# A mixture-of-experts and recurrence kernel: the recurrence's rotation moved from ScalarE and GpSimd to VectorE, y copied out of PSUM by ScalarE and added by GpSimd, the second routing in two halves

## The chip, the core and the metric

One core of a Trainium2 chip runs the whole program. The metric is the device time of one execution in microseconds (us), here the median of several runs. Engines are named as in the profile: PE (TensorE), PEld (its weight loads), DVE (VectorE), ACT (ScalarE), POOL (GpSimd), SP (SyncE, which only issues transfers here).

## The reference

The input x has 8 batches of 512 rows of 128 numbers. Three layers follow each other, each with a residual connection and each behind a layer norm:

```
x = x + 0.5 * ffn(layernorm(x), gate_w, w1, w2)
x = x + attn(layernorm(x), a_params, B_w, C_w, D)
x = x + 0.5 * ffn(layernorm(x), gate_w, w1, w2)

attn:  Bu = u @ B_w.T;  h_t = real(ifft(lambdas * fft(h_{t-1}))) + Bu_t;  y_t = h_t @ C_w.T + D * u_t
ffn:   logits = tokens @ gate_w;  probs = softmax(logits);  expert = argmax(probs)    # 8 experts
       place of a token = how many earlier tokens chose the same expert; places of 160 and more are dropped
       out = probs[expert] * (relu(token @ w1[expert]) @ w2[expert])
```

## The kernel before

**Frame.** The 4096 rows are 32 tiles of 128 rows, four tiles to a batch. The kernel is one block of hand-written programs, one for each engine, each strictly in its own order; only semaphores (`wait_ge`, `then_inc`) order the engines against each other. There is no scheduler. The program has five stages: the first routing (gate logits, one-hot tables, a matmul that turns them into a token list), the first expert stage `slots(0)` (gather ten tiles of 128 slots by indirect DMA, two products for each of 8 experts, scatter back into a scratch copy of x in DRAM), the recurrence over the 8 batches, the second routing, and `slots(1)`. The text calls the pass of the recurrence loops for batch i "turn i".

**The recurrence.** The transform diagonalises the recurrence, so that a state is a complex number for each frequency, its real parts on partitions 0 to 63 and its imaginary parts on 64 to 127. Four consecutive rows form a group, and a batch has 128 groups. For batch b: DVE takes the layer norm's statistics (`stats`, `shift`), ACT the standard deviation (`deviation`) and the normalised rows u (`normalise`, four instructions); PE transposes u (`turn_u`), ACT copies it to SBUF (`copy_uT`); PE forms the group sums v in `bank[5]` (`group_sums`). v is turned back by the angle of its group: va = v * cosine on DVE (`turn_back`), and vb = v with its halves exchanged * sine, for which ACT copies the two halves of v crosswise into `vq` (`turned_part`) and POOL multiplies. DVE runs a cumulative sum over va and vb into z (`carry`) and turns z forth again: zs on DVE, zc on POOL, and state = zc + zs on DVE (`turn_forth`). PE adds the contribution inside the groups (`within_pairs`, `within_rest`) and that of the carried state (`read_out`) in one pair of PSUM banks, `pair[b % 2]`. That PSUM tile holds y and, beside it, the terms of the gate logits of the second routing. DVE reads both from PSUM: `add_back` (x2 = y + x1, which SP then sends to the output) and `gate_back` (the logits).

**Second routing.** It works on pieces of batches, `PIECES[1]`, here 0 to 2, 3 to 5, and 6 and 7. For a piece DVE finds each token's expert and counts (`mark`), PE adds the counts over partitions and earlier pieces (`rank`), DVE makes one-hot tables (`make_hot`), and PE multiplies them into one small PSUM tile (`place`); DVE makes the token list of it (`index(1)`), and POOL gathers with it after all rows of x2 are in DRAM (`d_out`). `keep_warm` is n matmuls of 128x512 whose result nobody reads.

Two orders matter. ACT, in turn i: `turned_part(i)`, `copy_uT(i + 1)`, `deviation(i + 2)`, `normalise(i + 2)`. DVE, in turn i: `turn_back(i)`, `stats(i + 2)`, `carry(i)`, `turn_forth(i)`, `add_back(i - 1)`, `gate_back(i - 1)`, `shift(i + 2)`, and then a part of the routing.

## Time and profile before

| quantity | value |
|---|---|
| time, median of 3 runs | 175.39 us (174.82 to 181.41) |
| the profiled execution: its time | 176.61 us |
| its span (first to last instruction) | 174.7 us |
| busy share of the span | PE 80%, PEld 60%, DVE 51%, ACT 33%, POOL 30% |
| the chain that ended last, by engine | PE 41%, DVE 24%, issue 10%, ACT 8%, DMA 8%, POOL 5% |

The table's time is that of the whole program, and the span is measured inside it; 1.9 us of the profiled execution lie outside its span. A row of the time line gives the start in us from the span's start, the length in us, the engine, the line of the kernel, the operation with output and inputs, and in square brackets how long the engine had been idle and what released it. Names are cut at their first digit, so that x stands for x1 and x2, and pair for all of PSUM. "x4" at a row's end says that four instructions in a row are merged.

### The profile page before, as it was taken

Reading aid. Unit: us, or ns where it says so; the run is one execution under the profiler, and the core shown is the slowest. Engines: PE = TensorE matmul, PEld = TensorE weight load, DVE = VectorE, ACT = ScalarE, POOL = GpSimd, SP = SyncE. Lnnn points to the kernel's source line nnn. Section 1 sums busy time; section 2 is a strip of 40 time slices with the busy share of each in tenths; the row PEclk is TensorE's granted clock in tenths of the full one; section 3 lists DMA queues with packets and bytes.
Section 4 is the critical chain, followed back from the end, with each engine's and each line's share of the span. In section 5 each row is a group of like instructions: output and inputs, shape, how many; then the busy total and the mean of one; then the engine's idle time right before and its main releaser. Section 6 shows DMA issues by size and latency. Waiting matters only on the chain.

```text
span 174.7 us, 2535 instructions
## 1 busy us (share of the span) xinstructions
PE 140.6 (80%) x788; PEld 104.8 (60%) x791; DVE 89.7 (51%) x396; ACT 58.2 (33%) x144; POOL 52.9 (30%) x80
## 2 busy tenths in 40 slices
PE   6977899989999787499788888896439969999920
PEld 2137468389998432388566666675234448999810
DVE  1069762984474206065485597698464134434320
ACT  3421143634736000846525525510000013483200
POOL 3700001776047720022012012121000477305771
PEclk9998589999999999999999999999555987999995
DMA  4999990111001129300101100111010011100110
GB/s 133 314 364 362 372 560 19 45 45 51 9 19 58 51 51 323 141 2 0 60 25 39 60 38 23 62 60 64 0 60 0 13 47 45 45 4 31 46 45 30
DMA packets 11309, 16.21 MB, mean 93 GB/s; under 512 B 1665, under 2 KB 6273, under 8 KB 11265
## 3 DMA queue, kind: packets, MB, share of 16 engines
q1 hardware_dynamic: 9504, 13.11, 21.4%
q0 software_dynamic: 1280, 2.62, 5.0%
q10 hardware_dynamic: 512, 0.33, 0.7%
q8 instruction: 6, 0.10, 0.2%
q14 instruction: 7, 0.05, 0.1%
HBM read 12.65 MB, written 5.51 MB: 104 GB/s over the span
## 4 chain that ended last, share of the span: by engine, by line
PE 41%; DVE 24%; issue 10%; ACT 8%; DMA 8%; POOL 5%; SPq 1%; POOLq 1%; DVEq 0%; ACTq 0%
PE pair L910 11%; PE pair L921 9%; ACT u L440 5%; PE pair L852 5%; DVE sstat L701 4%; PE pair L879 4%; DMA xt<-x_turned 3%; PE pair L804 3%; DVE x L748 2%; PE pair L899 2%; POOL zc L344 2%; DVE smv L706 2%; DVE z L730 2%; DMA x<-x_scratch 2%; DMA xg<-out,tok 2%
## 5 line engine op out<-in xcount | busy, mean ns | idle before, releaser
L804 PE MATMUL pair<-warm_in,ones_bf 128*128 128x512 bf16 x77 | 21.7, 428 | 4.2 <-DVE warm_in L469 1.6
L910 PE MATMUL pair<-xcT,w1s 128*128 128x160 f32 x128 | 21.8, 316 | 0.0
L921 PE MATMUL pair<-hT,w2s 128*128 128x160 f32 x128 | 20.5, 303 | 0.8 <-ACT hT L394 0.8
L910 PEld LDWEIGHTS pair<-xcT,w1s 128*128 128x128 f32 x128 | 18.9, 199 | 0.8 <-ACT xcT L386 0.8
L394 ACT ACTIVATE hT<-pair 128x320 f32<-128x320 f32 x32 | 13.7, 436 | 16.4 <-PE pair L910 15.0
L921 PEld LDWEIGHTS pair<-hT,w2s 128*128 128x128 f32 x128 | 18.1, 192 | 1.5 <-ACT hT L394 0.8
L440 ACT ACTIVATE u<-x,snb,srs 128x128 f32<-128x128 f32 x32 | 13.2, 482 | 13.4 <-DVE snb L716 13.4
L317 POOL DMA_INDIRECT xg<-x,tok x10 | 10.2, 1024 | 23.7 <-DVE tok L638 20.9
L317 POOL DMA_INDIRECT xg<-out,tok x10 | 10.1, 1006 | 22.0 <-DVE tok L638 19.2
L804 PEld LDWEIGHTS pair<-warm_in,ones_bf 128*128 128x128 bf16 x80 | 8.3, 110 | 13.7 <-issue 3.3
L386 ACT COPY xcT<-pair 128x128 f32<-128x128 f32 x20 | 4.9, 266 | 31.3 <-PE pair L894 31.2
L339 POOL TENSOR_TENSOR vb<-vq,st 128x128 f32<-128x128 f32 x8 | 3.6, 455 | 37.3 <-ACT vq L420 37.3
L1020 PE MATMUL pair<-gt,state 128*128 128x272 f32 x32 | 10.4, 453 | 3.8 <-DVE state L743 3.8
L326 POOL DMA_INDIRECT out<-xnew,tok x10 | 9.9, 988 | 10.7 <-DVE xnew L682 8.9
L326 POOL DMA_INDIRECT x_scratch<-xnew,tok x10 | 9.9, 986 | 9.8 <-DVE xnew L682 7.9
L645 DVE BATCH_NORM_STATS2 gstat<-xg 128x6 f32<-128x128 f32 x20 | 5.7, 287 | 12.4 <-DMA xg<-out,tok 9.2
L879 PEld LDWEIGHTS pair<-hot_tok,hot_place 128*64 128x64 f16 x64 | 7.4, 202 | 7.8 <-DVE hot_place L623 6.1
L879 PE MATMUL pair<-hot_tok,hot_place 128*64 128x20 f16 x64 | 7.8, 265 | 5.3 <-DVE hot_place L623 5.3
L701 DVE BATCH_NORM_STATS2 sstat<-x 128x6 f32<-128x128 f32 x32 | 6.9, 278 | 6.9 <-DMA x<-x_scratch 6.9
L722 DVE TENSOR_TENSOR va<-pair,ct 128x128 f32<-128x128 f32 x8 | 2.3, 291 | 15.1 <-ACT vq L420 15.1
L672 DVE COPY eoT<-pair 128x160 f32<-128x160 f32 x16 | 5.1, 318 | 9.3 <-PE pair L921 9.3
L852 PE MATMUL pair<-w1s,center 128*128 128x512 f32 x16 | 9.6, 754 | 0.0
(170 smaller groups left out, 247.1 us busy)
## 6 DMA issues: line engine op xcount, KB each, us to landing
xt<-x_turned SPq DMA_DIRECT2D x8, 256.0 KB, 6.0
w1s<-w SPq DMA_DIRECT2D x2, 1024.0 KB, 7.5
w2s<-w SPq DMA_DIRECT2D x8, 256.0 KB, 6.7
x<-x_scratch SPq DMA_DIRECT2D x8, 256.0 KB, 4.5
out<-x SPq DMA_DIRECT2D x8, 256.0 KB, 2.0
ce<-const_early ACTq DMA_DIRECT2D x1, 318.0 KB, 4.4
cl<-const_late SPq DMA_DIRECT2D x1, 256.0 KB, 5.5
xg<-x,tok POOLq DMA_INDIRECT x10, 2.6
```

Source lines behind the costliest of these rows:

```text
L317: pool.indirect_dma_start(xg[:, j, :], None, (x_rows, out_rows)[n], bass.IndirectOffsetOnAxis(ap=tok[:, j:j + 1], axis=0), bounds_check=T ...
L326: pool.indirect_dma_start((x1_dram, out_rows)[n], bass.IndirectOffsetOnAxis(ap=tok[:, j:j + 1], axis=0), xnew[:, j, :], None, bounds_check ...
L394: nc.scalar.activation(hT[:, e % 2, half * HC:(half + 1) * HC, :], bank[4 + half][:, 0:HC * CAP] .rearrange("p (c s) -> p c s", c=HC), ACT ...
L440: ins = nc.scalar.activation(u[:, b % 2, c, :], x1[:, b * TB + c, :], ACT.Identity, bias=snb[:, b % 2, c:c + 1], scale=srs[:, b % 2, c:c + 1])
L645: link(V.bn_stats(gstat[:, j, :], xg[:, j, :]))
L701: ins = V.bn_stats(sstat[:, b % 2, c, :], x1[:, b * TB + c, :])
L804: M(bank[to][:, :], ones_bf[:, :], warm_in[:, :], start=True, stop=True)
L852: M(bank[e % 2][:, :], center[:, :], w1s[:, e, :], start=True, stop=True).then_inc(w1c_ps, 1)
L879: ins = M(bank[7][0:SW, 0:NSTRIP], hot_place[:, :, t], hot_tok[:, :, t], start=(t == 0), stop=(t == NT - 1))
L910: ins = M(bank[4 + half][:, c * CAP:(c + 1) * CAP], w1s[:, i, ch * P:(ch + 1) * P], xcT[:, i * CAP:(i + 1) * CAP], start=True, stop=True)
L921: ins = M(bank[6 + i % 2][:, 0:CAP], w2s[:, i, c, :], hT[:, i % 2, c, :], start=(c == 0), stop=(c == FC - 1))
L1020: ins = M(y[:, h, E:E + 2 * PITCH], state[:, b % 2, :], gt[:, 2 * h:2 * h + 2, :].rearrange("p r c -> p (r c)"), start=False, stop=True, s ...
```

## The change

In the recurrence, DVE computes vb itself: two instructions of 64 partitions each read v in PSUM and write the other half. ACT's two crosswise copies and POOL's product go; the cumulative sum subtracts vb. ACT gets a new step, `copy_y`, that copies y and the logit terms of a batch (128x576) from PSUM to SBUF (`yb`). `add_back` moves from DVE to POOL and `gate_back` stays on DVE, both now reading `yb`. On ACT `deviation` stands ahead of `copy_uT` instead of behind it. The second routing works on two pieces of four batches. The logits of the last batch no longer come out of its y: PE forms them by their own products (`gates_within`, `gates_carried`) from tables `tg` that POOL makes between its first gathers and first scatters (`first_tables`), and DVE reads them in `gate_first`. `keep_warm` ahead of `slots(1)` is one call of 14, in place of calls of 8 and 16 around the last `place`.

```diff
-    PIECES = [[(0, NB)], [(0, 3), (3, 6), (6, NB)]]
+    PIECES = [[(0, NB)], [(0, NB // 2), (NB // 2, NB)]]
+    LAST = NB - 1
+    YW = 2 * E + 2 * PITCH
...
-            return [(t0, (t0 + t1) // 2), ((t0 + t1) // 2, t1)] if n == 0 else [(t0, t1)]
+            return [(t0, (t0 + t1) // 2), ((t0 + t1) // 2, t1)]
...
-            for b in range(NB):
-                pool.wait_ge(vq_sb, b + 1)
-                if b >= 1:
-                    pool.wait_ge(z_r, b)
-                nc.gpsimd.tensor_tensor(vb[:, :], vq[:, :], st[:, 0:NG], ALU.mult).then_inc(vb_r, 1)
+            def first_tables():
+                pool.wait_ge(out_table, 1)
+                link(nc.gpsimd.memset(tg[:, :, :, :], 0.0))
+                for k in range(TB):
+                    nc.gpsimd.tensor_copy(tg[:, k, 0, k * E:].rearrange("p (j e) -> p j e", e=E),
+                                          tab[:, E:E + PITCH * (TB - k)].rearrange("p (j c) -> p j c", c=PITCH)
+                                          [:, :, D:PITCH])
+                    ins = nc.gpsimd.tensor_copy(tg[:, k, 1, k * E:(k + 1) * E], gate_c[:, 0:E])
+                ins.then_inc(first_table, 1)
...
+            def add_back(b):
+                pool.wait_ge(y_sb, b + 1)
+                nc.gpsimd.tensor_tensor(x2[:, b * TB:(b + 1) * TB, :].rearrange("p (h r) d -> p h r d", h=2),
+                                        y_copy(b)[:, :, :, 0:D],
+                                        x1[:, b * TB:(b + 1) * TB, :].rearrange("p (h r) d -> p h r d", h=2),
+                                        ALU.add).then_inc(x2_r, 1)
+            gather(0)
+            first_tables()
+            scatter(0)
+            pool.wait_ge(turns, 1)
+            for i in range(NB):
+                turn_cosine(i)
+                if i >= 1:
+                    add_back(i - 1)
+            add_back(LAST)
...
-            def turned_part(b):
-                act.wait_ge(v_ps, b + 1)
-                if b >= 1:
-                    act.wait_ge(vb_r, b)
-                v = bank[5][:, 0:NG]
-                nc.scalar.copy(vq[0:P // 2, :], v[P // 2:P, :])
-                nc.scalar.copy(vq[P // 2:P, :], v[0:P // 2, :]).then_inc(vq_sb, 1)
+            def copy_y(b):
+                act.wait_ge(y_ps, b + 1)
+                if b >= 2:
+                    act.wait_ge(x2_r, b - 1)
+                    act.wait_ge(y_read, b - 1)
+                nc.scalar.copy(yb[:, b % 2, :, :], y_pair(b)[:, :, 0:YW]).then_inc(y_sb, 1)
...
             for i in range(NB):
-                turned_part(i)
+                if i >= 1:
+                    copy_y(i - 1)
+                if i + 2 < NB:
+                    deviation(i + 2)
                 if i + 1 < NB:
                     copy_uT(i + 1)
                 if i + 2 < NB:
-                    deviation(i + 2)
                     normalise(i + 2)
+            copy_y(LAST)
...
             def turn_back(b):
-                dve.wait_ge(vq_sb, b + 1)
-                V.tensor_tensor(va[:, :], bank[5][:, 0:NG], ct[:, 0:NG], ALU.mult).then_inc(va_r, 1)
+                dve.wait_ge(v_ps, b + 1)
+                V.tensor_tensor(va[:, :], bank[5][:, 0:NG], ct[:, 0:NG], ALU.mult)
+                for src, dst in halves:
+                    ins = V.tensor_tensor(vb[dst, :], bank[5][src, 0:NG], st[src, 0:NG], ALU.mult)
+                ins.then_inc(va_r, 1)
...
+            def gate_first():
+                dve.wait_ge(first_ps, 1)
+                dve.wait_ge(y_read, LAST)
+                link(V.tensor_tensor(lgu[:, :, :], first[:, 1, :, :],
+                                     ssd[:, LAST % 4, :].unsqueeze(2).broadcast_to([P, TB, E]), ALU.mult))
+                V.tensor_tensor(lgs[:, LAST * TB:NT, :], first[:, 0, :, :], lgu[:, :, :], ALU.add).then_inc(y_read, 1)
...
-                if i == ROUTE_FROM:
+                if i == NB // 2:
                     mark(1, 0, (True, False))
-                if i == ROUTE_FROM + 1:
+                if i == NB // 2 + 1:
                     mark(1, 0, (False, True))
-                if i == ROUTE_FROM + 2:
-                    make_hot(1, 0, (True, False))
-                if i == ROUTE_FROM + 3:
-                    make_hot(1, 0, (False, True))
+                if i == NB // 2 + 2:
+                    make_hot(1, 0)
+            gate_first()
             mark(1, 1)
-            gate_back(NB - 1)
-            mark(1, 2)
-            add_back(NB - 1)
             make_hot(1, 1)
-            make_hot(1, 2)
             index(1)
...
+            def gates_within(b):
+                pe.wait_ge(first_table, 1)
+                pe.wait_ge(va_r, b + 1)
+                for k in range(TB):
+                    M(bank[5][:, 256:256 + 2 * TB * E], uT[:, b % 2, k * P:(k + 1) * P],
+                      tg[:, k, :, :].rearrange("p k c -> p (k c)"), start=(k == 0), stop=False, skip_group_check=True)
+            def gates_carried(b):
+                pe.wait_ge(state_r, b + 1)
+                M(first[:, 0, :, :], state[:, b % 2, :], gt[:, :, D:PITCH], start=False, stop=True,
+                  skip_group_check=True).then_inc(first_ps, 1)
...
+            group_sums(LAST)
+            read_out(LAST - 1)
+            gates_within(LAST)
+            gates_carried(LAST)
+            within_pairs(LAST)
+            within_rest(LAST)
             rank(1, 1)
-            read_out(NB - 1)
+            read_out(LAST)
+            place(1, 0)
             place(1, 1)
-            rank(1, 2)
-            keep_warm(8, 0)
-            place(1, 2)
-            keep_warm(16, 0)
+            keep_warm(14, 0)
             slots(1)
```

The order of ACT's instructions in turn 3, first before and then after. vq is the crosswise copy of v, yb the copy of y, ssd the deviation, uT the transposed u, u the normalised rows of the batch two turns ahead.

```order
L419 COPY vq<-pair 64x128 [waits vb_r,v_ps]
L420 COPY vq<-pair 64x128
L427 COPY uT<-pair 128x512 [waits lag_ps,uT_ps]
L433 ACTIVATE ssd<-smv,eps 128x4 [waits y_read,svar]
L440 ACTIVATE u<-x,snb,srs 128x128 [waits uT_ps,snb_r]
L440 ACTIVATE u<-x,snb,srs 128x128 x3
```

```order
L444 COPY yb<-pair 128x576 [waits y_read,x2_r,y_ps]
L457 ACTIVATE ssd<-smv,eps 128x4 [waits y_read,svar]
L451 COPY uT<-pair 128x512 [waits lag_ps,uT_ps]
L464 ACTIVATE u<-x,snb,srs 128x128 [waits uT_ps,snb_r]
L464 ACTIVATE u<-x,snb,srs 128x128 x3
```

The two copies that stood behind the preceding turn's u are gone, and no instruction of ACT stands between v and DVE any more.

DVE in turn 3, before and then after, from the first product on v to the first instruction of `gate_back`.

```order
L722 TENSOR_TENSOR va<-pair,ct 128x128 [waits vq_sb]
L701 BN_STATS sstat<-x 128x6 [waits d_x1_5]
...
L743 TENSOR_TENSOR state<-zc,zs 128x128 [waits y_ps,zc_r,zs_r]
L748 TENSOR_TENSOR x<-pair,x 128x512 [waits y_ps]
L758 TENSOR_TENSOR lgu<-pair,ssd 128x2x8 [waits y_ps]
```

```order
L751 TENSOR_TENSOR va<-pair,ct 128x128 [waits v_ps]
L753 TENSOR_TENSOR vb<-pair,st 64x128 x2
L728 BN_STATS sstat<-x 128x6 [waits d_x1_5]
...
L773 TENSOR_TENSOR state<-zc,zs 128x128 [waits y_ps,zc_r,zs_r]
L781 TENSOR_TENSOR lgu<-yb,ssd 128x2x8 [waits y_sb]
```

The first product waits for PE's sums instead of ACT's copy, two products of 64 partitions are new, and the 128x512 addition is gone.

PE from the group sums of the last batch to the first product of the last piece's one-hot tables, before and then after. counted belongs to `rank`, hot_tok and hot_place to `place`, tg to `gates_within`.

```order
L1020 MATMUL pair<-gt,state 128x272 [waits state_r]
...
L1012 MATMUL pair<-tab,uT 128x144
L879 MATMUL pair<-hot_tok,hot_place 64x20 [waits hot]
L879 MATMUL pair<-hot_tok,hot_place 64x20 x11
L864 MATMUL pair<-counted_0,ones_bf 128x96 [waits rank_read,marked]
...
L1020 MATMUL pair<-gt,state 128x272 [waits state_r]
L1020 MATMUL pair<-gt,state 128x272
L879 MATMUL pair<-hot_tok,hot_place 64x20 [waits hot]
L879 MATMUL pair<-hot_tok,hot_place 64x20 x11
L864 MATMUL pair<-counted_0,ones_bf 128x64 [waits rank_read,marked]
```

```order
L1054 MATMUL pair<-tg,uT 128x64 [waits va_r,first_table]
L1054 MATMUL pair<-tg,uT 128x64 x3
L1060 MATMUL pair<-gt,state 128x32 [waits state_r]
L1021 MATMUL pair<-tab,uT 128x280 [waits y_sb]
...
L1036 MATMUL pair<-tab,uT 128x144
L889 MATMUL pair<-counted_0,ones_bf 128x128 [waits rank_read,marked]
...
L1044 MATMUL pair<-gt,state 128x272 [waits state_r]
L1044 MATMUL pair<-gt,state 128x272
L904 MATMUL pair<-hot_tok,hot_place 64x20 [waits hot]
L904 MATMUL pair<-hot_tok,hot_place 64x20 x7
```

The small gate products now stand ahead of the last batch's other products and wait for its state, the last `rank` stands ahead of the last `read_out`, and every `place` of the second routing stands behind it.

## Rows read from the trace of the kernel before

**Rows 1.** Time line of DVE, va of turn 3, then turn 4.
```profile
93.52 0.29 DVE L722 TENSOR_TENSOR va<-pair,ct 128x128 f32<-128x128 f32 x1 [2.27 <-ACT vq L420]
...
100.05 0.29 DVE L722 TENSOR_TENSOR va<-pair,ct 128x128 f32<-128x128 f32 x1 [1.89 <-ACT vq L420]
100.26 0.86 DVE L701 BATCH_NORM_STATS2 sstat<-x 128x6 f32<-128x128 f32 x4
...
101.45 0.39 DVE L730 TENSOR_TENSOR_SCAN z<-va,vb 128x128 f32<-128x128 f32 x1
101.87 0.75 DVE L734 TENSOR_TENSOR zs<-z,st 64x128 f32<-64x128 f32 x2
102.66 0.29 DVE L743 TENSOR_TENSOR state<-zc,zs 128x128 f32<-128x128 f32 x1
102.86 0.68 DVE L748 TENSOR_TENSOR x<-pair,x 128x512 f32<-128x512 f32 x1
103.46 0.25 DVE L758 TENSOR_TENSOR lgu<-pair,ssd 128x16 f32<-128x16 f32 x2
...
104.06 0.16 DVE L716 SCALAR_TENSOR_TENSOR snb<-smv,srs 128x4 f32<-128x4 f32 x1
```

**Rows 2.** Time line of ACT, end of turn 3 and turn 4.
```profile
97.74 1.65 ACT L440 ACTIVATE u<-x,snb,srs 128x128 f32<-128x128 f32 x4 [2.40 <-DVE snb L716]
99.41 0.26 ACT L419 COPY vq<-pair 64x128 f32<-64x128 f32 x1
...
100.13 0.59 ACT L427 COPY uT<-pair 128x512 f32<-128x512 f32 x1 [0.19 <-PE pair L977]
101.56 0.30 ACT L433 ACTIVATE ssd<-smv,eps 128x4 f32<-128x4 f32 x1 [0.84 <-DVE smv L706]
```

**Rows 3.** Time line of PE, group sums of turns 1 and 2, and the read out between.
```profile
76.86 1.05 PE L986 MATMUL pair<-uT,vt 128*128 128x128 f32 x8
78.11 1.18 PE L1020 MATMUL pair<-gt,state 128*128 128x272 f32 x4 [0.20 <-DVE state L743]
...
81.92 1.05 PE L986 MATMUL pair<-uT,vt 128*128 128x128 f32 x8
```

**Rows 4.** Time line of DVE behind the last turn.
```profile
118.64 0.29 DVE L743 TENSOR_TENSOR state<-zc,zs 128x128 f32<-128x128 f32 x1
...
124.37 0.26 DVE L758 TENSOR_TENSOR lgu<-pair,ssd 128x16 f32<-128x16 f32 x2 [2.47 <-PE pair L1020]
...
131.55 0.23 DVE L604 TENSOR_TENSOR own_count<-pair,chosen 128x64 f32<-128x64 f32 x1 [1.95 <-PE pair L871]
...
135.95 0.17 DVE L631 TENSOR_SCALAR unfilled<-pair 64x20 f32<-64x20 f32 x1 [2.25 <-PE pair L879]
```

**Rows 5.** Time line of PE behind the last turn.
```profile
122.19 2.15 PE L1020 MATMUL pair<-gt,state 128*128 128x272 f32 x4
...
131.73 3.19 PE L804 MATMUL pair<-warm_in,ones_bf 128*128 128x512 bf16 x7 [0.22 <-issue]
```

**Rows 6.** Busy time by stretch: PE, PEld, DVE, ACT, POOL, granted clock, DMA, GB/s.
```profile
122.00:123.00 1.00, 1.00 (x6) 0.88 (x7) 0.00 (x0) 0.00 (x0) 0.00 (x0) 0.53 0.00 0
```

**Rows 7.** Groups by form on POOL: busy us, mean ns, idle before.
```profile
L344 POOL TENSOR_TENSOR zc<-z,ct 128x128 f32<-128x128 f32 x8 | 4.5, 559 | 10.5 <-DVE z L730 10.5
L339 POOL TENSOR_TENSOR vb<-vq,st 128x128 f32<-128x128 f32 x8 | 3.6, 455 | 37.3 <-ACT vq L420 37.3
```

**Rows 8.** Groups by form on DVE, columns as in rows 7.
```profile
L551 DVE TENSOR_TENSOR chosen<-key,top_key 128x128 bf16<-128x128 bf16 x2 | 1.4, 716 | 0.1
L623 DVE TENSOR_TENSOR hot_place<-split_i,place_no 128x512 f16<-128x512 int16 x1 | 0.4, 416 | 0.0
```

**Rows 9.** The chain that ended last, first routing: start, us, what.
```profile
24.37 3.63 PE pair L879 x32
```

**Rows 10.** Time line of POOL, the first scatter.
```profile
49.94 1.01 POOL L326 DMA_INDIRECT x_scratch<-xnew,tok  x1 [7.04 <-DVE xnew L682]
```

**Rows 11.** The page's list of DMA issues: count, KB each, us to landing.
```profile
out<-x SPq DMA_DIRECT2D x8, 256.0 KB, 2.0
```

50 lines of the change are left out of this document (19 added, 31 removed).

## The prediction

> **What bounds the kernel now.** I read the chain of waits first. Outside the two expert stages, which the diff leaves alone, it runs through the recurrence and the second routing; so I read the time lines of the engines there.
>
> *A turn of the recurrence* takes 6.53 us, from the va of turn 3 at 93.52 to that of turn 4 at 100.05, and DVE stood idle for 1.89 us before the latter, released by ACT's vq copy [rows 1]. ACT was late because vq stands behind the four u instructions of batch 5 (97.74, 1.65 us), and these had waited 2.40 us for DVE's snb [rows 2]. The snb of a turn comes last on DVE, 104.06 + 0.16 = 4.17 us behind its va [rows 1]. So the turn is one ring: va, statistics, z, zs, state, x2, logits, snb on DVE (4.2 us), then u and vq on ACT (2.3 us). The reader is to see that v itself has long been ready; the ring closes only because ACT is strictly in order.
>
> *PE's own work* in a turn is shorter. From the group sums of turn 1 (76.86) to those of turn 2 (81.92) are 5.06 us with 0.20 us of waiting for the state [rows 3]: 4.9 us of work. A turn therefore wastes some 1.6 us.
>
> *Behind the last turn* the state is ready at 118.64 + 0.29 = 118.93, and the token list starts at 135.95 [rows 4]: 17.0 us. DVE waits three times there for PE: 2.47 us for the last read_out, 1.95 us for the last rank, 2.25 us for the last place [rows 4]. The read_out took 2.15 us at a granted clock of 0.50 to 0.53, PE's lower level of 1.2 GHz, against 1.18 us at 2.4 GHz [rows 3, 5, 6], and eight keep_warm products (3.19 us for seven recorded) still ran when the last one-hot table was done [rows 5].
>
> **The change part by part.**
>
> *Out of the ring.* va now waits for PE's sums alone. Then what comes last in a turn? DVE's turn from the row starts [rows 1]: va 0.21, statistics to z 1.19, z 0.42, zs 0.79, state 0.20, then (x2's 0.60 is gone) logits and shift 0.60 to the start of snb and some 0.08 until the next instruction starts: 3.5 us. New is vb, two products of 64 partitions out of PSUM. The trace has no such pair; the nearest are the two zs, 64 partitions crosswise, 0.75 us [rows 1], and va, 0.29 us for 128 partitions out of PSUM, started 0.21 us apart. So 0.42 to 0.85 us; I take 0.70, nearer to zs, as that is the same crosswise form. DVE: 4.2 us. ACT: y copy of 576 columns at the uT copy's rate, 0.59 x 576 / 512 = 0.66, deviation 0.30, uT 0.59, u 1.65 [rows 2]: 3.2 us. POOL: zc 0.56 and x2, four times the columns of a product that takes 0.455 alone and 0.559 beside DVE's zs [rows 7]: 1.2 (part of the 0.455 is start-up) to 2.24 us, so 1.8 to 2.8 us. PE's 4.9 us is the largest, and **PE bounds the turn**.
>
> Do the orders allow it? Counted from the group sums of turn i: sums done 1.05, va to svar until 3.1, snb until 5.2, u of batch i + 2 until 6.9. PE wants that u for its transposes 3.4 us into the next turn, at 8.3: 1.4 us to spare. The state is ready at 4.5 or so and wanted at 1.05 of the next turn, 5.95. The read_out of the turn before ends at 2.25, the y copy at 2.95, deviation (behind svar) at 3.4, the transposes of u at 4.0, the uT copy at 4.65, wanted at 4.9. That last one has the least to spare, 0.25 us. What is queued behind the y copy on ACT is deviation, uT and u; behind deviation's wait stands uT. Only in turn 0 does this show: deviation there comes later than uT's wait and pushes it by some 0.25 us. POOL's x2 starts at 4.1 and ends at 6.3 at the latest, before the next z at 8.4.
>
> So group sums of turn 1 at 77.1, of turn 5 at 77.1 + 4 x 4.9 = 96.7.
>
> *Routing inside the loop.* The first piece now has 16 tiles instead of 12. Turn 4 gets two small instructions (0.6 us), which DVE's spare 0.7 us takes. Turn 5 gets the choice: 0.72 for `chosen` [rows 8], its neighbours some 0.25, 0.3 and 0.4, 1.7 us in all, and from there DVE is last. Its va of turn 5 is at 96.7 + 1.1 = 97.8; with 4.2 and 1.7 turn 6 starts at 103.7. Turn 6 has no statistics: 2.8 us, then the whole make_hot. Two hot_place at 0.42 [rows 8] and nine small ones of 0.1 to 0.4 make 2.85. Turn 7 starts at 109.35; va and vb 1.0 with their wait, z 0.46, zs 0.79 and state 0.29 [rows 1] make the state of batch 7 ready at **111.9**, where it was 118.9: 7.0 us gained.
>
> *Behind the state.* gates_carried on PE 0.35 (read_out's four large products take 1.18 [rows 3], so this one small one at most a third), gate_first 0.45 (two instructions like lgu's, each waited for [rows 1]), mark on 16 tiles 2.4 (the 0.6 and 1.7 from above with their waits), all in a row: 115.1. PE does the products inside the groups meanwhile (2.4 us) and is free at about 114.7. rank, four small products and no row of that size here: between 0.3 and half of read_out, taken as 0.5: 115.6. Now two branches. DVE: make_hot, 2.85, done at 118.45. PE: read_out 1.1 to 116.7, then place of all 32 tiles, 3.63 in the first routing [rows 9], to **120.35**. PE is last. Before, 17.0 us lay between the state and the list; now 8.45.
>
> *Other work that is moved.* first_tables stands on POOL ahead of the first scatter, where POOL idled for 7.04 us [rows 10]. It is nine instructions of 8 to 256 columns, under 0.3 us each: at most 2.7 us, hidden; its cover is the wait for the first expert's rows. The x2 of batch 7 now goes y copy on ACT (0.66), POOL (1.2 to 2.24), then the transfer that lands after 2.0 us [rows 11]: 116.7 + 0.05 + 0.66 + 1.7 + 2.07 = 121.2. The gathers also need the list itself, 0.9 us behind 120.35, at 121.25. So it is hidden by nothing to spare; at POOL's upper bound it costs 0.5 us. Before, that transfer was long done.
>
> *POOL beside DVE.* zc takes 0.559 beside DVE's zs, vb 0.455 without [rows 7], and the two zs together take 0.75 where two starts 0.29 apart would give 0.6 [rows 1]. x2 on POOL now lies beside state, logits and snb in each turn and beside turn 7's. In the turns DVE has room; in the chain from turn 5 on I add 0.4 us. The Trainium skill (GPSIMD Engine Reference, Specifications) says that POOL's SBUF interface is shared with VectorE and that they contend when the VectorE instruction has two SBUF inputs; its section on engine selection advises against elementwise work with two inputs on GpSimd. The rows fit with that: both sides are longer where they overlap. By that rule the 0.4 us stays; were the overlap free, the sum would be 0.4 us lower.
>
> **Sum.** 135.95 - 120.35 = 15.6 gained, less 0.4: 15.2 us. Everything behind the list is unchanged in the diff but for fewer warming products. The profiled execution of 176.61 us would take 161.4. It was 1.2 us above the median of the runs, 175.39, so for a median I forecast **160.4 us**.
>
> **Rivals.**
>
> *A, the clock.* PE's clock was at its lower level from 122 on [rows 6], behind two microseconds in which PE had nearly no work. In the changed kernel PE works without a gap until about 109, then waits for DVE's turn 7, does 0.5 us of gate products and waits again until 112.2. If the level falls there, the products inside the groups take 4.8 instead of 2.4 us and end at 117.1 instead of 114.7; rank then is 1.5 us later, read_out takes 1.0 us more [rows 3, 5], and the sum loses some 2.5, perhaps 4 with what the warming takes: 163.5. For it: nearly 2.5 us of idling in a stretch of 3. Against it: in the turns before, PE idled 1.3 us of each 6.5 and kept its clock.
>
> *B, a longer turn.* Another wait takes the ring's place: ACT's uT copy, which has 0.25 us to spare, or DVE slowed by POOL. A turn of 5.6 instead of 4.9 costs 0.7 x 5 = 3.5 us: 164. For it: 0.25 us is little, and waits between engines cost some 0.05 each. Against it: no single row contradicts the times.
>
> *C, faster still.* vb at its lower bound and the overlap free give 0.3 x 3 + 0.4 = 1.3 us; and the warming products end nearer to the first gathered tile, so that the expert stage may start at the full clock: 1 us or so. 158.5.
>
> *D, slower than before.* POOL becomes the bound: x2 is a product of 512 columns, and if DVE keeps POOL from SBUF much more than zc shows, a turn is zc plus x2. It breaks even when seven turns give back 15.2 us, that is a turn of 4.9 + 2.2 = 7.1 us and an x2 of 6.5 us, three times its upper bound of 2.24 [rows 7]. At 8 us for x2 the time would be about 186. Only a contention of which no row shows a sign would do it.
>
> *E, the gate products bring nothing.* The last mark would wait as before for the last y: 2.4 + 1.1 us behind the state instead of 0.35, less what rank no longer has to wait: about 2.5 us, 163. The order shows that they stand ahead, so only their table or the bank they share could delay them.
>
> **How the numbers follow.** The forecast as worked out has 0.55, A 0.17, B 0.14, C 0.09, E 0.03, D 0.02. The likeliest is the forecast: 160.4. For the range, C's end and the bounds of vb and x2 below (158.3), and A and B above, with one and a half us for both at once: 165.5. Two per cent, about what a measurement of this kernel can tell from no change, is 3.5 us; every case but D is faster by far more. Faster 0.96, same 0.02, slower 0.02.
>
> **What would show it.** Right: va released by PE's sums, not by ACT; group sums some 4.9 us apart with PE idle under 0.3 us a turn; DVE last from turn 5; list at about 120 to 121; place right behind read_out with no keep_warm between; x2 on POOL 1.2 to 2.2 us. Wrong: a turn over 5.4 us (B), granted clock 0.5 between 111 and 118 (A), gathers that start later than 0.9 us behind the list because the last output is still on its way.

## The result, and the profile after

The changed kernel took 168.26 us (median of four runs, 166.73 to 169.68) against 176.44 us for the kernel before beside it: a ratio of 0.9528, 95% interval [0.9456, 0.9601]. Four more executions of it on another occasion gave 168.04 us and 0.9464 [0.9355, 0.9574]. It is faster by 5%, where 8.5% were forecast; 168.26 lies above the range. The profiled execution took 166.96 us with a span of 165.1, so it is compared with the forecast of 161.4: 5.6 us are missing.

The time line of DVE in turns 2 and 3 of the changed kernel (columns as in [rows 1], which these answer):

```profile
77.10 0.29 DVE L773 TENSOR_TENSOR state<-zc,zs 128x128 f32<-128x128 f32 x1
...
83.96 0.28 DVE L751 TENSOR_TENSOR va<-pair,ct 128x128 f32<-128x128 f32 x1
84.26 0.59 DVE L753 TENSOR_TENSOR vb<-pair,st 64x128 f32<-64x128 f32 x2
...
86.51 0.76 DVE L764 TENSOR_TENSOR zs<-z,st 64x128 f32<-64x128 f32 x2
87.30 1.25 DVE L773 TENSOR_TENSOR state<-zc,zs 128x128 f32<-128x128 f32 x1
...
89.15 0.28 DVE L751 TENSOR_TENSOR va<-pair,ct 128x128 f32<-128x128 f32 x1
```

and that of POOL beside it:

```profile
86.55 0.56 POOL L351 TENSOR_TENSOR zc<-z,ct 128x128 f32<-128x128 f32 x1 [3.34 <-DVE z L761]
87.08 1.32 POOL L356 TENSOR_TENSOR x<-yb,x 128x512 f32<-128x512 f32 x1
...
123.60 1.29 POOL L356 TENSOR_TENSOR x<-yb,x 128x512 f32<-128x512 f32 x1 [6.72 <-ACT yb L444]
```

The ring is gone: va follows at once, where it had waited for vq [rows 1]. But the turn is 5.19 us (83.96 to 89.15), and DVE has no idle time in it: DVE bounds it, not PE. One row grew. The addition that makes `state` takes 1.25 us in every turn with an x2 beside it, and 0.29 us in turn 0 (77.10), the only one without. It ends at 88.55, 0.15 us behind the end of POOL's x2 at 88.40. (The profile calls its times on POOL rough; experiments 2 to 5 show whether this distance holds for other instructions.)

PE of the changed kernel, group sums of turns 1, 2 and 7, the read_out behind the first of them and products behind the last; then its clock by stretch (columns as in [rows 6]):

```profile
77.68 1.05 PE L1011 MATMUL pair<-uT,vt 128*128 128x128 f32 x8
78.57 1.08 PE L1044 MATMUL pair<-gt,state 128*128 128x272 f32 x4
...
82.28 1.05 PE L1011 MATMUL pair<-uT,vt 128*128 128x128 f32 x8
...
109.20 1.05 PE L1011 MATMUL pair<-uT,vt 128*128 128x128 f32 x8
...
114.66 1.94 PE L1054 MATMUL pair<-tg,uT 128*128 128x64 f32 x8 [2.88 <-DVE vb L753]
...
117.53 1.28 PE L1021 MATMUL pair<-tab,uT 128*128 128x280 f32 x2
...
121.50 0.22 PE L889 MATMUL pair<-counted,ones_bf 128*128 128x128 bf16 x1
```
```profile
74.00:78.00 4.00, 4.00 (x19) 3.46 (x18) 3.47 (x17) 1.17 (x3) 0.49 (x1) 0.71 0.01 2
...
114.00:117.00 3.00, 1.94 (x8) 1.78 (x8) 2.87 (x7) 0.00 (x0) 1.83 (x2) 0.50 0.00 0
120.00:122.00 2.00, 2.00 (x13) 1.69 (x13) 0.66 (x3) 0.00 (x0) 0.00 (x0) 0.84 0.03 8
```

Unhindered, PE's turn is 4.60 us (77.68 to 82.28). In turn 7 PE had waited 2.88 us for DVE, and its clock stood at the lower level, 1.2 GHz, so that its products inside the groups ended only near 121.5. In 74 to 78 the clock had also been low for a part.

DVE behind the last turn of the changed kernel, answering to [rows 4]:

```profile
115.79 1.24 DVE L773 TENSOR_TENSOR state<-zc,zs 128x128 f32<-128x128 f32 x1
...
121.91 0.29 DVE L631 TENSOR_TENSOR own_count<-pair,chosen 128x128 f32<-128x128 f32 x1 [1.31 <-PE pair L896]
...
123.42 0.33 DVE L645 TENSOR_TENSOR hot_strip<-split_i,strip_no 128x320 f16<-128x320 int16 x1
123.78 1.29 DVE L647 TENSOR_TENSOR hot_tok<-hot_strip,token_half 128x320 f16<-128x320 f16 x1
...
127.43 0.17 DVE L658 TENSOR_SCALAR unfilled<-pair 64x20 f32<-64x20 f32 x1 [1.70 <-PE pair L904]
```

`hot_tok`, of the size of `hot_strip` (0.33 us), takes 1.29 us, because x2 of the last batch lies beside it (123.60 to 124.89). The list starts at 127.43. The first gather starts 1.76 us behind it (129.19), where it was 1.75 before; so the last output doesn't hold the gathers up, and the 0.9 us that the prediction took for this step were too few in both kernels.

Traces differ by a microsecond or three in when the recurrence begins, for reasons upstream of the diff. So from here on the yardstick is the **stage**: from the start of the recurrence's first statistics on DVE to the start of the list (`unfilled`). Before it was 135.95 - 66.53 = 69.42 us; changed, 127.43 - 65.68 = 61.75; forecast, 120.75 - 66.53 = 54.2. That is a gain of 7.7 where 15.2 were forecast; 0.85 and 1.1 us came from upstream and from behind the list.

| profiled execution | stage | to the last state | state to list | turn | state | group sums 0 to 1 |
|---|---|---|---|---|---|---|
| before | 69.42 | 52.11 | 17.31 | 6.45 | 0.29 | 3.78 |
| forecast | 54.2 | 45.1 | 9.1 | 4.9 | | |
| changed | 61.75 | 50.11 | 11.64 | 5.19 | 1.25 | 5.46 |
| changed, again (12) | 61.78 | 49.05 | 12.73 | 5.18 | 1.24 | 4.27 |
| changed, warmed ahead of the tail (8) | 63.00 | 51.41 | 11.59 | 5.18 | 1.25 | 6.43 |
| changed, first turn warmed (11) | 61.79 | 49.06 | 12.73 | 5.19 | 1.25 | 4.26 |
| x2 on DVE (1) | 58.87 | 49.14 | 9.73 | 4.84 | 0.29 | 6.61 |
| the same without own gate products (7) | 60.24 | 49.12 | 11.12 | 4.84 | 0.29 | 6.48 |
| x2 later on POOL (2) | 57.47 | 46.92 | 10.55 | 4.60 | 0.29 | 4.26 |
| x2 in four on POOL (3) | 58.20 | 47.98 | 10.22 | 4.87 | 0.43 | 5.47 |
| x2 and tables later (9) | 57.94 | 47.00 | 10.94 | 4.60 | 0.29 | 6.50 |
| the same, first turn warmed (10) | 54.35 | 44.66 | 9.69 | 4.60 | 0.29 | 4.26 |
| rotation alone (6) | 63.21 | 47.14 | 16.07 | 4.83 | 0.29 | 5.46 |
| before, dose on POOL (4) | 73.85 | 57.05 | 16.80 | 7.17 | 1.01 | 5.47 |
| before, copy on POOL (5) | 70.44 | 54.03 | 16.41 | 6.74 | 0.58 | 3.78 |

"To the last state" and "state to list" split the stage at the start of the last `state`; the turn is turn 2, from va to va; the numbers in brackets are those of the experiments. The last column tells TensorE's clock in the first turn. At 3.78 (kernel before) and 4.3 us it was full. At 5.5 us it was at the lower level for some 3 us, and at 6.4 to 6.6 us for some 6. Rows with a like last column can be compared. Some executions of every kernel run at a lower granted clock and take longer: the medians below count them, the ratios leave them out, and the profiled executions of experiments 1, 7 and 9 are such (167.28, 169.09 and 167.59 us), which shows ahead of the first statistics and in the first turn.

### The profile page after: what moved, and what is told of

Same layout as the page of the kernel before. It is cut to its first block, busy times and chain, and to the rows that moved or that the text cites. A ratio compares the mean times of both kernels' runs of the same rounds, so it can differ in the third digit from the quotient of the medians.

```text
span 165.1 us, 2502 instructions
## 1 busy us (share of the span) xinstructions
PE 140.3 (85%) x783; PEld 107.7 (65%) x786; DVE 95.4 (58%) x389; ACT 58.3 (35%) x136; POOL 60.7 (37%) x87
## 4 chain that ended last, share of the span: by engine, by line
PE 40%; DVE 28%; issue 9%; POOL 9%; DMA 8%; ACT 2%; POOLq 1%; SPq 0%; DVEq 0%
PE pair L935 8%; PE pair L946 8%; PE pair L877 5%; DVE state L773 5%; DVE sstat L728 4%; POOL xg L321 4%; PE pair L904 3%; DMA xt<-x_turned 3%; POOL zc L351 2%; DVE vb L753 2%; PE pair L924 2%; DMA x<-x_scratch 2%; PE pair L849 2%; DMA xg<-out,tok 2%; DVE z L761 2%
## 5 line engine op out<-in xcount | busy, mean ns | idle before, releaser
L829 PE MATMUL pair<-warm_in,ones_bf 128*128 128x512 bf16 x67 | 19.0, 431 | 4.3 <-DMA x<-x_scratch 1.6
L935 PE MATMUL pair<-xcT,w1s 128*128 128x160 f32 x128 | 20.7, 305 | 0.0
L351 POOL TENSOR_TENSOR zc<-z,ct 128x128 f32<-128x128 f32 x8 | 4.4, 551 | 41.9 <-DVE z L761 41.9
L935 PEld LDWEIGHTS pair<-xcT,w1s 128*128 128x128 f32 x128 | 18.0, 190 | 0.8 <-ACT xcT L411 0.8
L829 PEld LDWEIGHTS pair<-warm_in,ones_bf 128*128 128x128 bf16 x70 | 7.4, 111 | 13.3 <-issue 4.0
L356 POOL TENSOR_TENSOR x<-yb,x 128x512 f32<-128x512 f32 x8 | 10.5, 1309 | 6.7 <-ACT yb L444 6.7
L1044 PE MATMUL pair<-gt,state 128*128 128x272 f32 x32 | 9.3, 414 | 1.1 <-DVE state L773 0.8
L444 ACT COPY yb<-pair 128x576 f32<-128x576 f32 x8 | 5.0, 624 | 14.0 <-PE pair L1044 14.0
L1011 PE MATMUL pair<-uT,vt 128*128 128x128 f32 x64 | 9.0, 285 | 0.7 <-ACT uT L451 0.7
L709 DVE SCALAR_TENSOR_TENSOR xnew<-pair,gscale,xg 128x128 f32<-128x128 f32 x20 | 6.4, 346 | 5.3 <-PE pair L955 5.2
```

The lines of the kernel that those rows point to most:

```text
L356: nc.gpsimd.tensor_tensor(x2[:, b * TB:(b + 1) * TB, :].rearrange("p (h r) d -> p h r d", h=2), y_copy(b)[:, :, :, 0:D], x1[:, b * TB:(b + ...
L829: M(bank[to][:, :], ones_bf[:, :], warm_in[:, :], start=True, stop=True)
L935: ins = M(bank[4 + half][:, c * CAP:(c + 1) * CAP], w1s[:, i, ch * P:(ch + 1) * P], xcT[:, i * CAP:(i + 1) * CAP], start=True, stop=True)
L1011: ins = M(bank[5][:, 0:NG], vt[:, TB - 1 - c, :], uT[:, b % 2, c * P:(c + 1) * P], start=(c == 0), stop=(c == TB - 1))
L1044: ins = M(y[:, h, E:E + 2 * PITCH], state[:, b % 2, :], gt[:, 2 * h:2 * h + 2, :].rearrange("p r c -> p (r c)"), start=False, stop=True, s ...
```

## The experiments

Each median stands beside runs of the kernel before on the same chip. Diffs are cut to the lines that matter, with `...` for what is left out inside a line or between lines.

**1. x2 on DVE.**

```diff
             def add_back(b):          # moved from POOL's program to DVE's
-                pool.wait_ge(y_sb, b + 1)
-                nc.gpsimd.tensor_tensor(x2[...], y_copy(b)[...], x1[...], ALU.add).then_inc(x2_r, 1)
+                dve.wait_ge(y_sb, b + 1)
+                V.tensor_tensor(x2[...], y_copy(b)[...], x1[...], ALU.add).then_inc(x2_r, 1)
...
             make_hot(1, 1)
+            add_back(LAST)
```

> x2 of every batch back on DVE (reading the copy yb), the rest of the change kept; the last x2 stands behind the last make_hot. Theory H (hold): a DVE instruction with two inputs in SBUF that is issued while POOL runs its 128x512 addition ends only when that addition has ended; in the changed kernel this made state 1.25 us long instead of 0.29 and hot_tok 1.29 instead of 0.32. H expects state at 0.29 us and hot_tok at 0.32 in this run; DVE loses 0.95 and regains 0.60 per turn, so the turn falls from 5.19 to about 4.85 us, turns 5 to 7 give 0.35 each, the last table 0.7: time 2 to 3 us below the changed kernel's 166.9, about 164.5. Rival R (the length of state has another cause, such as its inputs or the semaphores it waits for): state stays at 1.25 us and the turn grows by 0.60, time about 171. Rival S (shared rate: DVE and POOL each run slower while both read SBUF): state 0.29 as well, but see the run with four small additions.

Measured: 163.69 us, ratio 0.9283 [0.9179, 0.9387]. DVE's time line of this kernel:

```profile
91.35 0.29 DVE L763 TENSOR_TENSOR state<-zc,zs 128x128 f32<-128x128 f32 x1
91.56 0.69 DVE L768 TENSOR_TENSOR x<-yb,x 128x512 f32<-128x512 f32 x1
...
97.69 0.28 DVE L741 TENSOR_TENSOR va<-pair,ct 128x128 f32<-128x128 f32 x1
```

`state` is back at 0.29 us and the last `hot_tok` at 0.33, and the turn is 4.84 (the va before stands at 92.85) although DVE does one more instruction of 0.69: moving x2 to POOL cost DVE more (0.95) than the 0.60 us that it saved. The stage is 2.9 us shorter than in the changed kernel's first trace, although the first turn's clock was worse. Against experiment 8, the changed kernel with a like first turn, it is 4.1 us shorter.

**2. x2 on POOL, but later**: behind snb of its turn, so that it runs beside the next va, vb and statistics; the last one on DVE.

```diff
                 turn_cosine(i)
+                if 1 <= i and i + 2 < NB:
+                    pool.wait_ge(snb_r, i + 3)
+                if i + 2 == NB:
+                    pool.wait_ge(rank_read, piece(1, 0) + 1)
+                if i + 1 == NB:
+                    pool.wait_ge(y_read, LAST)
                 if i >= 1:
                     add_back(i - 1)
-            add_back(LAST)
...
             make_hot(1, 1)
+            add_last(LAST)     # DVE: the x2 of the last batch
```

> x2 stays on POOL but starts later: in turns 1 to 5 behind DVE's snb, so that it lies beside va, vb and the statistics, which read at most one input from SBUF; in turn 6 behind own_count, in turn 7 behind gate_back; the last x2 is on DVE behind the last make_hot. H expects state at 0.29 us in every turn, none of va, vb or the statistics longer than before, DVE's turn 4.2 us and PE the bound at 4.7 to 4.9 us a turn; 0.3 to 0.5 us for each of turns 2 to 5, 0.95 for each of turns 5 to 7, 0.7 behind the last rank: time 4 to 5 us below the changed kernel, about 162.5. S expects that the time which state loses comes back on va, vb and the statistics, so a turn of 5.1 us and a time within 1 us of the changed kernel. R expects no change of state and no gain.

Measured: 164.0 us, ratio 0.93 [0.9156, 0.9444]. POOL and DVE of this kernel, turns 3 and 4, then three rows of the routing:

```profile
92.87 1.27 POOL L356 TENSOR_TENSOR x<-yb,x 128x512 f32<-128x512 f32 x1 [1.24 <-DVE snb L748]
...
97.47 1.27 POOL L356 TENSOR_TENSOR x<-yb,x 128x512 f32<-128x512 f32 x1 [1.24 <-DVE snb L748]
```
```profile
91.81 0.29 DVE L778 TENSOR_TENSOR state<-zc,zs 128x128 f32<-128x128 f32 x1
...
93.06 0.29 DVE L756 TENSOR_TENSOR va<-pair,ct 128x128 f32<-128x128 f32 x1 [0.27 <-PE pair L1025]
93.37 0.59 DVE L758 TENSOR_TENSOR vb<-pair,st 64x128 f32<-64x128 f32 x2
93.99 0.87 DVE L733 BATCH_NORM_STATS2 sstat<-x 128x6 f32<-128x128 f32 x4
...
97.62 1.27 DVE L573 TENSOR_TENSOR is_top<-lgs,top 128x128 bf16<-128x128 f32 x1
...
103.92 1.43 DVE L583 TENSOR_TENSOR chosen<-key,top_key 128x128 bf16<-128x128 bf16 x1
...
109.21 0.93 DVE L640 TENSOR_SCALAR over<-count 128x16 f32<-128x16 f32 x1
```

Now va has to wait 0.27 us for PE, and a turn is 4.60 us: PE bounds it, as forecast, and faster than forecast. Beside va and vb (one input in PSUM) and the statistics (one input; all of them lie beside x2 in turn 5 of experiment 10), POOL's x2 lengthens nothing: 0.29, 0.59 and 0.87 us as without. Where it meets `is_top`, with two inputs in SBUF, that takes 1.27 instead of 0.29, and again ends just behind it (98.89, and 98.74). `chosen` (1.43 for 0.70) and `over` (0.93 for 0.17, one input in SBUF) are held too, so part of the gain is lost in the routing. They don't end 0.15 us behind POOL (104.77 and 110.11) but 0.58 and 0.03. What is common to all of them is the difference: each ends its own unhindered time, less 0.12 to 0.14 us, behind the end of POOL's instruction. A held instruction thus does nearly all of its work afterwards. The stage is 4.3 us shorter than that of experiment 12, the changed kernel with the same full clock in the first turn.

**3. x2 on POOL as four additions of 128x128** in the place of one.

```diff
-                nc.gpsimd.tensor_tensor(x2[...], y_copy(b)[:, :, :, 0:D], x1[...], ALU.add).then_inc(x2_r, 1)
+                for h in range(2):
+                    for r in range(2):
+                        ins = nc.gpsimd.tensor_tensor(x2[:, b * TB + 2 * h + r, :], y_copy(b)[:, h, r, 0:D],
+                                                      x1[:, b * TB + 2 * h + r, :], ALU.add)
+                ins.then_inc(x2_r, 1)
```

> x2 on POOL at its place in the changed kernel, but as four additions of 128x128 instead of one of 128x512. H, if the hold lasts for one POOL instruction: state gets in between two of them and takes 0.3 to 0.8 us instead of 1.25; the turn falls by 0.3 us or more to PE's bound, time 1.5 to 3.5 us below the changed kernel, 163.5 to 165.5. S expects state unchanged at 1.1 to 1.3 us, since the same number of elements is read, and the time unchanged or up to 1 us longer for the added starts.

Measured: 166.86 us, ratio 0.9482 [0.9159, 0.9805]; the interval is wide, the trace is clear. POOL, then DVE:

```profile
87.41 1.81 POOL L358 TENSOR_TENSOR x<-yb,x 128x128 f32<-128x128 f32 x4
```
```profile
87.63 0.43 DVE L774 TENSOR_TENSOR state<-zc,zs 128x128 f32<-128x128 f32 x1
87.98 0.51 DVE L782 TENSOR_TENSOR lgu<-yb,ssd 128x16 f32<-128x16 f32 x2
```

POOL reads the same data for longer, 1.81 us, yet DVE loses less: `state` 0.43, lgu 0.51 for 0.25. So DVE isn't slowed in proportion to POOL's traffic; it is kept out until the instruction in hand ends, and gets in between two. The stage is 3.6 us shorter than in the changed kernel's first trace, whose first turn was alike.

**4. The dose on the kernel before**: a POOL addition of 128x512 behind each zc, whose result nobody reads.

```diff
                 nc.gpsimd.tensor_tensor(zc[:, :], z[:, 0:NG], ct[:, 0:NG], ALU.mult).then_inc(zc_r, 1)
+                nc.gpsimd.tensor_tensor(spare[:, :, :], x1[:, b * TB:(b + 1) * TB, :], x1[:, b * TB:(b + 1) * TB, :],
+                                        ALU.add)
```

> The kernel before, with one more instruction on POOL in each turn: a 128x512 addition of two SBUF operands into a tile that nobody reads, right behind zc, so that it lies beside DVE's state. Theory H (a VectorE instruction with two SBUF inputs issued beside it ends only when it has ended): state goes from 0.29 to about 1.25 us in all 8 turns though nothing waits for POOL's result; the ring grows by 0.95 and the time by 0.95 x 8 = 7.6 us, 6.5 to 8. Rival S (shared rate): state 0.4 to 0.6 and the time 1 to 3 us longer. Rival R (state is long in the changed kernel for a reason of its own): no change of state and of the time.

Measured: 181.78 us (179.53 to 186.51) beside 177.95 for the kernel before (175.81 to 179.59), less than expected; stage 139.84 - 65.99 = 73.85. DVE and POOL:

```profile
90.58 1.01 DVE L746 TENSOR_TENSOR state<-zc,zs 128x128 f32<-128x128 f32 x1
```
```profile
90.36 1.08 POOL L346 TENSOR_TENSOR spare<-x 128x512 f32<-128x512 f32 x1
```

One instruction without a reader makes `state` 1.01 us and the turn 7.17 (va at 87.97 and 95.14) instead of 6.45: both are 0.72 us longer. Up to the last `state` there are seven such turns, 5.0 us, and the trace is 4.9 us longer there. The expected 7.6 us took the dose for as long as x2; it is 0.2 us shorter, and the part behind the last `state` is 0.5 us shorter than before, since the clock fell later there (DVE waits 1.60 us for the last read_out instead of 2.47). The hold needs nothing else of the change.

**5. A copy in place of that addition**, one input instead of two.

```diff
-                nc.gpsimd.tensor_tensor(spare[:, :, :], x1[:, b * TB:(b + 1) * TB, :], x1[:, b * TB:(b + 1) * TB, :],
-                                        ALU.add)
+                nc.gpsimd.tensor_copy(spare[:, :, :], x1[:, b * TB:(b + 1) * TB, :])
```

> The kernel before, with one more POOL instruction behind each zc: a copy of 128 x 512 values of x1 into a spare tile, that is, one input where the addition of the earlier dose had two. Its result is used by nobody. Theory H (any POOL instruction on this much data keeps DVE out while it runs): state takes 0.29 us plus what is left of the copy, near 1 us, as beside the addition (1.01 us). Theory T (POOL has to read two inputs for it): state stays at 0.29 us, and the turns at 6.5 us, as in the kernel before.

Measured, one execution: 177.72 us beside 176.67.

```profile
96.75 0.67 POOL L346 COPY spare<-x 128x512 f32<-128x512 f32 x1
```
```profile
96.98 0.58 DVE L745 TENSOR_TENSOR state<-zc,zs 128x128 f32<-128x128 f32 x1
```

The copy is shorter than I had allowed for, and `state` again ends 0.14 us behind it (97.56, and 97.42). It is 0.29 us longer than alone; seven times that is 2.0 us, and up to the last `state` the trace is 1.9 us longer. Theory H holds as against T: a copy with one input holds `state` as an addition does, for as long as it runs.

**6. The rotation alone**: the kernel before with vb on DVE, without ACT's copies and POOL's product, and without the rest of the change.

```diff
-                turned_part(i)
...
-                dve.wait_ge(vq_sb, b + 1)
-                V.tensor_tensor(va[:, :], bank[5][:, 0:NG], ct[:, 0:NG], ALU.mult).then_inc(va_r, 1)
+                dve.wait_ge(v_ps, b + 1)
+                V.tensor_tensor(va[:, :], bank[5][:, 0:NG], ct[:, 0:NG], ALU.mult)
+                for h in range(2):
+                    src, dst = slice((1 - h) * P // 2, (2 - h) * P // 2), slice(h * P // 2, (h + 1) * P // 2)
+                    ins = V.tensor_tensor(vb[dst, :], bank[5][src, 0:NG], st[src, 0:NG], ALU.mult)
+                ins.then_inc(va_r, 1)
```

> The kernel before with one part of the change: DVE computes vb out of PSUM in two instructions, ACT's crosswise copies and POOL's product are gone; x2 stays on DVE out of PSUM, the routing stays in three pieces. Theory P (the ring over ACT was the bound): the turn falls from 6.5 to 4.7 to 4.9 us, DVE's work of 4.8 us beside PE's of 4.6 to 4.9, and since no POOL addition lies beside state this one part alone gains 8 to 10 us, as much as the whole change does: 166 to 168. Rival: freeing DVE of x2 was the needed part, and DVE with vb and x2 has turns of 5.3 us or more, a gain under 6 us.

Measured: 169.57 us, ratio 0.9532 [0.9424, 0.964]; stage 128.93 - 65.72 = 63.21. This part alone gives what the whole change gives, within the intervals. Up to the last `state` it is 3.0 us quicker than the changed kernel, at the same low clock in the first turn; behind it 4.4 us slower. So what the change does for the second routing gains behind the turns. Of the 3.0 us that it loses in them, the holds account for 2.1 to 2.3 (experiments 1 and 2 up to the last `state`, against 8 and 12); the rest isn't assigned by any run. Turn 2 falls from 6.45 to 4.83 us, and DVE has no idle time in it: with x2 still on DVE, DVE bounds the turn and not PE.

**7. The last batch's logits out of its y again**, on the kernel with x2 on DVE.

```diff
-            gate_first()
+            dve.wait_ge(y_read, LAST)
+            gate_back(LAST)
...
-            gates_within(LAST)
-            gates_carried(LAST)
...
-            rank(1, 1)
             read_out(LAST)
+            rank(1, 1)
```

> The kernel with x2 on DVE, but the last batch's logits come out of its y again: gates_within and gates_carried go, read_out of the last batch stands ahead of the last rank, and gate_back(LAST) takes the place of gate_first. Theory P (the own gate products bring what they were forecast to, since the last mark no longer waits for y): own_count of the last half comes some 2.5 to 3 us later behind the last state than in the run with x2 on DVE (there 5.12 us behind the start of state), the list as well, and the median goes from 163.7 to about 166.3. Theory E (they bring nothing, PE's products inside the groups decide anyway): own_count and the median stay within 0.5 us.

Measured: 165.23 us, ratio 0.9322 [0.9238, 0.9406], against 0.9283 with the products: 1.5 us in the medians, inside both intervals. Its trace has own_count 6.51 us behind the last `state`:

```profile
118.37 0.29 DVE L763 TENSOR_TENSOR state<-zc,zs 128x128 f32<-128x128 f32 x1
...
121.30 0.26 DVE L779 TENSOR_TENSOR lgu<-yb,ssd 128x16 f32<-128x16 f32 x2 [1.64 <-ACT yb L434]
...
124.88 0.29 DVE L621 TENSOR_TENSOR own_count<-pair,chosen 128x128 f32<-128x128 f32 x1 [0.68 <-PE pair L897]
```

With the products it was 123.08 - 117.96 = 5.12. So they bring some 1.4 us, neither 2.5 to 3 nor nothing. Without them DVE waits for y only 1.64 us, because PE has done the products inside the groups before the state comes (the last ends at 116.44). Both tails had the lower clock for a part, this one longer (its read_out took 1.81 us, 1.08 at full clock), so at one clock it would be less.

**8. Twelve warming products behind the last but one read_out**, in the changed kernel, for PE's waiting ahead of its gate products.

```diff
             read_out(LAST - 1)
+            keep_warm(12, 4)
             gates_within(LAST)
```

> The changed kernel with keep_warm(12) on PE between read_out of batch 6 and gates_within, where PE idled for 2.88 us and its granted clock then was 0.50 until 121. Theory C (the lower clock cost time in the tail): the clock stays at 1.0 until the last rank, gates_within takes 0.9 instead of 1.94 us, the products inside the groups 2.6 instead of 4.0, the last rank no longer waits for them (DVE idles 0.5 instead of 1.31 us before own_count): the time falls by 0.8 to 1.5 us. Rival: the tail is set by DVE alone, and the time does not change by more than 0.3 us; or the warming products run into the gate products and cost up to 0.5 us.

Measured: 172.25 us, ratio 0.9747 [0.9563, 0.9931]. PE and its clock (of PE alone: length, busy time, granted clock, DMA share, GB/s):

```profile
120.44 1.08 PE L1054 MATMUL pair<-tg,uT 128*128 128x64 f32 x8 [0.30 <-DVE vb L753]
122.86 0.41 PE L1060 MATMUL pair<-gt,state 128*128 128x32 f32 x2 [1.35 <-DVE state L773]
...
123.90 1.11 PE L1023 MATMUL pair<-tab,uT 128*128 128x272 f32 x2
```
```profile
120.00:123.00 3.00, 1.35 (x11) 1.00 0.00 0
123.00:126.00 3.00, 3.00 (x10) 0.57 0.25 93
```

The gate products now run at full clock (1.08 for 1.94 us), but they did so without the warming as well, in experiments 11 and 12. But PE waits 1.35 us more for the `state` that POOL holds up, and then the clock falls for the products inside the groups. own_count comes 6.07 us behind the start of `state`, 6.12 without the warming: nothing gained there. The stage was 63.0, with the first turn at half clock, and the first statistics were 4.5 us later (70.16) than in the changed kernel, upstream of the edit. This is time lost ahead of the edit, so the slower median can't be put down to the warming; why all four executions (171.08 to 176.15) are slower than seven of the changed kernel's eight (166.73 to 169.68, the eighth 171.60), one trace can't say. Theory C fell: filling that one gap doesn't keep the clock.

**9. x2 later, and the second half of the first piece's tables behind the last mark.** On the kernel of experiment 2, with x2 of batch 3 waiting for the next va instead of snb:

```diff
-                    make_hot(1, 0)
+                    make_hot(1, 0, (True, False))
...
             mark(1, 1)
+            make_hot(1, 0, (False, True))
             make_hot(1, 1)
```

> The changed kernel with x2 moved as in the earlier run, the one of turn 4 now beside the statistics of turn 5, and with the first piece's make_hot cut in two: own_count to split_i in turn 6, the tables themselves behind the last mark, where DVE idled 1.3 to 1.9 us for the last rank. Theory: the state of batch 7 is ready 1.5 us earlier, PE idles 1.5 us less before its gate products, the wait for the last rank is filled; 1.5 to 2.5 us faster than the run with x2 moved alone, about 161.5 to 162.5. Rival: PE's lower clock in the tail returns the gain, since the last rank waits for PE's products: less than 0.5 us.

Measured: 165.5 us, ratio 0.9236 [0.9099, 0.9373]. The stage was 57.94, against 57.47 in experiment 2, but here the first turn ran at the lower clock and there at the full one. Experiment 10 gives the fair comparison: the same schedule with a full first turn reaches the last `state` in 44.66 us, experiment 2 in 46.92. Of these 2.3 us, 1.0 come from the x2 of batch 3, which no longer holds `is_top` (from the state of turn 4 to that of turn 5 are 4.89 us for 5.86), and 1.3 from the later tables (5.03 us for 6.31 from turn 6 to 7). The expectation was 1.5.

**10. The same kernel with 22 instead of 14 warming products ahead of the first turn.**

```diff
             pe.wait_ge(d_x1[0], 16)
-            keep_warm(14, 6)
+            keep_warm(22, 6)
             turn_u(0)
```

> The kernel with x2 later on POOL and its tables behind the last mark (median 165.5 in its run), with 22 instead of 14 warming products ahead of the first turn, so that PE works until the first u is ready instead of idling some 2 us. Theory W (the idling of those 2 us is what lets the granted clock fall in the first turn): the first group sums take 1.16 us or less in place of 2.08, group sums 1 start 4.3 us behind group sums 0 instead of 6.5 (4.26 and 6.50 are the two that earlier runs showed), and the median falls to about 163. Theory U (the clock falls by what happened earlier, whatever PE does in those 2 us): the first turn shows 0.50 to 0.6 again in this run where it did in the others, and the median stays at 164 to 165.5.

Measured: **160.88 us**, ratio 0.9101 [0.903, 0.9173], the fastest of all; its six runs span 160.41 to 163.49. PE, DVE and the clock:

```profile
67.03 4.92 PE L846 MATMUL pair<-warm_in,ones_bf 128*128 128x512 bf16 x22 [1.55 <-DMA x<-x_scratch]
...
73.56 1.16 PE L1028 MATMUL pair<-uT,vt 128*128 128x128 f32 x8 [0.68 <-ACT uT L458]
```
```profile
111.67 0.29 DVE L780 TENSOR_TENSOR state<-zc,zs 128x128 f32<-128x128 f32 x1
...
116.79 0.28 DVE L638 TENSOR_TENSOR own_count<-pair,chosen 128x128 f32<-128x128 f32 x1
...
121.36 0.17 DVE L665 TENSOR_SCALAR unfilled<-pair 64x20 f32<-64x20 f32 x1 [1.09 <-PE pair L921]
```
```profile
114.00:117.00 3.00, 2.17 (x14) 1.44 (x12) 2.86 (x9) 0.00 (x0) 0.00 (x0) 1.00 0.23 87
```

The first group sums take 1.16 us. Up to the last `state` the kernel is 2.3 us quicker than in experiment 9, and the clock stays full in the tail until the last tables, another 1.25 us. The stage is 54.35 us, where 54.2 was forecast for the changed kernel; as this one has its x2 and tables elsewhere, that is a coincidence.

The numbers are those of theory W. But another thing separates the traces as well: when the recurrence begins. Six profiled executions have their first statistics between 66.4 and 67.3 us, four with 14 warming products (before at 66.53, experiment 5 at 66.51, 12 at 66.88, 2 at 67.26) and the two with 22 (11 at 66.49, 10 at 67.01), and all six have the full clock in the first turn. The eight that begin earlier (65.68 to 66.31) or later (68.82 to 70.20) have the lower one, and all of these have 14. No trace has 22 products and another beginning. So what the eight more products do to the clock isn't shown; that the median fell from 165.5 us to 160.9 on another chip speaks for them, but weakly: the intervals of the two ratios still overlap.

**11. Those 22 warming products in the changed kernel itself.** The diff is that of experiment 10.

> The changed kernel itself, x2 on POOL right behind zc as it is, with 22 instead of 14 warming products ahead of the first turn, and nothing else. Theory W (PE's idling ahead of the first turn lets the clock fall there): group sums 1 start 4.3 us behind group sums 0, the clock of the first 8 us of the turns is 1.00, and the median is some 1 to 2 us under the 168 us of the changed kernel, 166.5, because the turns behind it are still DVE's 5.19 us. If warming alone were what made the run with it and the later x2 fast (160.9 us), it would be 163 here. Theory Z (warming changes nothing where DVE bounds the turns): 168.

Measured: 169.27 us (167.31 to 170.79) beside 177.6; 167.86 in its profiled execution; stage 128.28 - 66.49 = 61.79. The first turn has the full clock, group sums 1 come 4.3 us behind group sums 0, and the last `state` comes 1.05 us sooner than in the changed kernel's first trace. But the time doesn't fall, as theory Z had it, for a reason that neither names: the tail is 1.09 us longer, since the products inside the groups and those of the last `rank` run at 1.2 GHz:

```profile
116.84 0.64 PE L1060 MATMUL pair<-gt,state 128*128 128x32 f32 x2 [1.35 <-DVE state L773]
117.29 1.28 PE L1021 MATMUL pair<-tab,uT 128*128 128x280 f32 x2
```

Experiment 12, the same kernel with 14 products, gives the same trace to 0.01 us in every column of the table. So warming gained nothing here, and alone it isn't what makes experiment 10 fast.

**12. The changed kernel again**, unedited, as a yardstick beside 4, 6 and 9.

> The changed kernel itself, unaltered, beside the next three on one chip, as their yardstick: about 167 us, from the first statistics to the token list 61.7 us as in its first profile.

Measured: 168.04 us, ratio 0.9464 [0.9355, 0.9574]. Its first turn had the full clock, its tail half clock from 0.6 us behind the start of `state` on (own_count 123.09 - 115.93 = 7.16 us behind it), and its stage was 61.78: as in 11, what it won at one end it lost at the other.

## Why the prediction was wrong

**The ring, right.** va is released by PE or follows at once; the rotation alone takes turn 2 from 6.45 to 4.83 us. vb cost 0.59 (taken: 0.70).

**PE bounds the turn, wrong in the changed kernel.** DVE's turn was put at 4.2 us and is 5.19. Of the difference 0.95 is the hold of `state`. Without it, x2 later on POOL, PE does bound the turn, at 4.60 us. Its work had been put at 4.9, 5.06 less 0.20 of waiting [rows 3]. But the read_out starts there 1.25 us behind the group sums, and 0.89 where nothing hinders it (77.68 and 78.57 above): the wait for the state had cost 0.36.

**"POOL beside DVE", the step that failed.** It stood in the sum with 0.4 us for the whole kernel. The right mechanism was named, even with its condition, but priced as a slight slowing, from zc's 0.559 against 0.455 us. It is a wait until POOL's instruction ends: 0.95 us for each `state` of turns 1 to 7, and 0.97 for the last `hot_tok`. Set beside the forecast's marks, with 0.85 us added for the earlier start: group sums 1 at 78.5 (77.1 forecast, 1.4 of it the low clock of the first turn), group sums 5 at 98.7 (96.7), va of turn 5 at 101.0 (97.8, DVE being last from turn 2 on), state of batch 7 at 117.9 (111.9), list at 128.3 (120.35). Of these 7.9 us, some 6.0 are there before the state and the rest behind it, there by the clock and `hot_tok`. The holds account for the turn's pace and for 0.95 in each of turns 5 to 7; in the first turns DVE had slack over PE's pace, so they can't simply be added up. Taking the holds away gains 4.1 us of the stage (x2 on DVE against experiment 8) to 4.3 (x2 later against experiment 12), each beside a changed kernel with a like first turn: ten times the 0.4. Of the 7.5 us by which the stage exceeds its forecast these are 3.8, the first turn's clock is 1.1 (below) and that of the tail some 0.9 (rival A); 1.7 us are assigned by no run.

Priced as such a wait, the step would have held. With the 1.2 to 2.24 us that the prediction gave x2, its start 0.2 us ahead of `state` and the 0.14 us of overlap, the hold is 0.9 to 1.9 us and DVE's 4.2 us become 5.1 to 6.1, an estimate from these rows; measured was 5.19.

The Trainium skill states how long such a wait lasts, on a page that the prediction didn't use: SBUF — State Buffer, "Who interferes with whom" and "SBUF: two separate sides". There the pair of ports that VectorE and GpSimd share is an exclusive lock, held for a whole instruction, and issue order decides who waits. A VectorE instruction contends there if it has two SBUF inputs or runs in a two-port mode; with at most one SBUF input, outside those modes, it does not. The traces agree on VectorE's side: `state`, `is_top`, `chosen` and `hot_tok` are held to the end of POOL's instruction, `over`, a tensor_scalar in SBUF, is held too, and va, vb and the statistics are not. Of the other order, VectorE first, they show little: zc, which starts 0.04 us behind the first zs, took 0.56 us for 0.455.

**Rival B, right in kind.** "DVE slowed by POOL" was given 0.14, at 5.6 us a turn and 164 us; it was 5.19 us a turn. Its price left out that DVE is last from turn 5 on anyway, with three more holds, and `hot_tok`.

**Rival A came as well.** The clock fell where it said: 0.50 from 114 to 117 and 0.84 in 120 to 122. Its price was smaller than the 2.5 us it gave: DVE waits 1.31 us for the last rank, which at full clock takes some 0.4 (experiment 10: the counts are ready at 115.6, the rank's last product ends at 116.07), so some 0.9 us here, and 2.0 in experiments 11 and 12, where the clock fell later and rose later. That the hold of `state` is what lets the clock fall isn't shown. PE waits 1.35 us for the held `state` in 8, 11 and 12 and 0.41 in experiment 1. But the clock fell in the tail of experiments 1, 2 and 9 too, with no hold there, and it stayed full in 10, whose schedule is that of 9.

**The gate products** bring some 1.4 us at most, forecast near 2.5 (rival E: nothing). **The first turn's clock** was in neither sum nor range, since the profile before had it full; it costs 1.1 us where it was low for some 3 us (50.11 against 49.05 to the last `state`, changed kernel) and 2.3 where it was low for some 6 (47.00 against 44.66 in 9 and 10, where PE bounds the turn, and 51.41 against 49.05 in 8 and 12, where DVE does).

**The list to the end**: 1.1 us shorter than before, forecast unchanged. Open stays what sets the clock between 20 and 40 us: the traces with the lowest clock there (1, 7, 8 and 9, 0.50 in 28 to 32) begin the recurrence at 68.8 to 70.2, the others at 65.7 to 67.3.

## What to carry to other kernels

Work moved from VectorE to GpSimd is free here only beside VectorE instructions with an input in PSUM and beside the statistics; those with two SBUF inputs were held, and one tensor_scalar with a single one. Write down which VectorE instruction starts while it runs, and charge that one GpSimd's whole remaining time. A large GpSimd instruction on the cyclic path is then better placed behind a semaphore that starts it beside such instructions (here 4.3 us of the stage), or cut into pieces (3.6), or left on VectorE (4.1, at 0.69 us each). A dose whose result nobody reads, on the old kernel, tests such a price before anything is moved.
And a microsecond won at one place can be lost at another through TensorE's clock, so compare stages of the trace, at the same clock, before believing a median. A condition that was meant to change the clock (here more warming) is only tested if the traces beside it begin alike.

## What the runs showed of the hardware

- A held VectorE instruction ends its own unhindered time, less 0.12 to 0.14 us, behind GpSimd's instruction: `over` (0.17 us alone) 0.03, `state` and `is_top` (0.29) 0.15, `hot_tok` (0.32) 0.18, `chosen` (0.70) 0.58. With GpSimd at 1.32, 1.08 and 0.67 us, `state` took 1.25, 1.01 and 0.58 us.
- GpSimd's addition of 128x512 fp32 takes 1.27 to 1.32 us from two tensors, 1.08 us of one tensor with itself, a copy 0.67 us; on VectorE the addition takes 0.69. Four additions of 128x128 take 1.81.
- TensorE's clock fell to 1.2 GHz for some time in the first turn of eight of the twelve profiled executions with 14 warming products, behind 2.0 us without work for PE (at worst group sums took 2.08 us for 1.16), and in neither of the two in which eight more products filled that time. But those two began the recurrence where all four with 14 products and a full clock did, between 66.4 and 67.3 us.
